# Two feed-forwards joined with the norms and the projection in front of them, in a four-block cross-attention network

## The reference

```python
def _L0_xattn_ref(...):
    ...                                   # x = x + causal self and context attention of _ln(x)
    hdn = _ln(_ln(x, g2, be2), gf, bf) @ w1 + b1          # w1: 256 x 1024
    hdn = jax.nn.gelu(hdn, approximate=False)
    x = x + (hdn @ w2 + b2)                               # w2: 1024 x 256
...
def _L3_xattn_ref(...):
    ...                                   # out = attention over ctx_1024
    attention = out @ w_out + b_out
    x = layernorm(attention + query, g1, beta1)
    ff = jax.nn.relu(x @ w_ff1 + b_ff1) @ w_ff2 + b_ff2
    return layernorm(ff + x, g2, beta2)
```

## Time and profile before

| what | value |
|---|---|
| median of 3 runs | 1797.35 us (1794.04 to 1807.53) |
| profiled execution | 1802.82 us, its span 1801.1 us |
| TensorE busy | 1422.7 us, 79% of the span |
| VectorE, ACT, GpSimd busy | 1046.8, 746.6, 514.5 us |
| mean granted TensorE clock | 0.873 of full speed |

### The profile page before, as it was taken

The page is one execution under the profiler, slowest core; times in us unless marked ns, Lnnn a source line. Parts: engine busy times, 40 slices in busy tenths (PEclk is TensorE's granted clock), DMA queues, the critical chain, the costliest instruction groups (busy, mean ns, idle before and its releaser), DMA issues. The chain is left out here.

```text
span 1801.1 us, 23058 instructions
## 1 busy us (share of the span) xinstructions
PE 1422.7 (79%) x7752; PEld 833.6 (46%) x7752; DVE 1046.8 (58%) x2359; ACT 746.6 (41%) x1044; POOL 514.5 (29%) x304
## 2 busy tenths in 40 slices
PE   5869998999369878769889668598895777587597
...
DMA packets 78127, 110.40 MB, mean 61 GB/s; under 512 B 16383, under 2 KB 55481, under 8 KB 76217
## 3 DMA queue, kind: packets, MB, share of 16 engines
...
...
## 5 line engine op out<-in xcount | busy, mean ns | idle before, releaser
L1036 PE MATMUL banks<-stacks 128*128 128x512 f32 (+4 forms) x640 | 252.9, 429 | 61.3 <-SPq L262 21.3
L1163 ACT ACTIVATE x_feat<-banks,key_bias 128x1024 f32<-128x1024 f32 x160 | 176.6, 1113 | 287.8 <-PE banks L1075 229.2
L1001 POOL TENSOR_TENSOR x_feat<-x_feat 128x1024 f32<-128x1024 f32 x112 | 265.6, 2372 | 87.5 <-ACT x_feat L1163 81.1
L1090 PE MATMUL banks<-x_feat,v_group 128*64 128x512 f32 (+4 forms) x1312 | 235.4, 574 | 10.1 <-ACT x_feat L1163 6.9
L1163 ACT ACTIVATE x_feat<-banks 128x1024 f32<-128x1024 f32 (+3 forms) x224 | 180.3, 839 | 142.8 <-PE banks L1069 93.5
L1206 DVE TENSOR_REDUCE max_parts<-banks 128x1 f32<-128x512 f32 (+3 forms) x384 | 192.9, 552 | 24.2 <-PE banks L1040 12.7
L1036 PEld LDWEIGHTS banks<-stacks 96*128 96x128 bf16 (+1 forms) x640 | 92.3, 148 | 239.9 <-DVE max_parts L1206 87.3
L1066 PE MATMUL banks<-stacks 99*128 99x512 bf16 (+3 forms) x512 | 141.1, 349 | 13.5 <-DMA stacks<-neg_max_parts 6.0
L1200 DVE CUSTOM_DVE_ANT_0 scratch<-banks,mask_rows 128x512 f32<-128x512 f32 x128 | 88.4, 691 | 67.4 <-PE banks L1036 67.2
L1074 PE MATMUL banks<-stacks 128*128 128x512 f32 x256 | 112.5, 440 | 7.1 <-DMA stacks<-neg_max_parts_r 7.1
L434 POOL TENSOR_TENSOR y_tok<-y_tok,rows_even 128x1024 f32<-128x1024 f32 x4 | 9.6, 2407 | 377.8 <-ACT y_tok L444 377.8
...
## 6 DMA issues: line engine op xcount, KB each, us to landing
...
```

What stands on the lines that cost most here:

```text
L1001: e.tensor_tensor(total, total, p, ALU.add)
L1036: m = e.matmul(PS[:, bank, at:at + wide], q[0:rows, h, qt * P:(qt + 1) * P], keys[0:rows, h, k0:k0 + wide], start=True, stop=not diag, ski ...
L1090: m = e.matmul(PS[w * h:w * (h + 1), bank, t.q0:CH], V[:, h, :], PB[:, t.index % 2, h // 2, h % 2, 0:CH - t.q0], start=t.first, stop=t.las ...
L1163: e.activation(dst, PS[:, 2 * (st % 2):2 * (st % 2) + 2, 0:CH - t.q0], ACT.Exp, scale=A.scale, bias=bias).then_inc(s.p_ready, 1)
```

## The change

Each of the two feed-forwards becomes one stage with what stands in front of it: three barriers fewer. Only chunk 0 goes through norms and transposes before the first hidden product (in the last block the projections of chunks 0 and 1, and the norm of chunk 0). What later chunks need is called by a function `between(c, m)` of each engine, after the step m of chunk c. Transposes and projections there use bank 3 alone, one at a time; the hidden products rotate over banks 0 to 2. The weight splits go in halves, and GpSimd's subtraction in pieces of 512 columns. The final norm's square root stands behind step 4 instead of 5, its normalisation behind 5 instead of 6. The context products' second pair moves to banks 4 and 5. The diff, cut to its core:

```diff
 
-    def split_weights_scalar(e, s, w):
-
-        for i in range(8):
+    def split_high(e, s, w, half):
+
+        for i in range(4 * half, 4 * half + 4):
             a = slice(CH * i, CH * (i + 1))
             h = e.activation(W_H[:, a], w[:, a], ACT.Copy)
         h.then_inc(s.w_high, 1)
 
-    def split_weights_gpsimd(e, s, w):
-        e.wait_ge(s.w_high, 1)
-        e.tensor_tensor(W_L, w, W_H.bitcast(F32), ALU.subtract)
-
-    def split_tokens_scalar(e, s, c):
+    def split_low(e, s, w, half):
+
+        e.wait_ge(s.w_high, half + 1)
+        for i in range(4 * half, 4 * half + 4):
+            a = slice(CH * i, CH * (i + 1))
+            h = e.tensor_tensor(W_L[:, a], w[:, a], W_H[:, a].bitcast(F32), ALU.subtract)
+        h.then_inc(s.w_low, 1)
+
+    def split_tokens_scalar(e, s, tn, c):
 
         if c < NC:
+            e.wait_ge(tn.taken, KT * (c + 1))
             need(e, s.hid_product, (c - 1) * MT_F)
             e.activation(XH[:, c % 2], XTF[:, :, c * CH:(c + 1) * CH], ACT.Copy).then_inc(s.x_high, 1)
 
@@ -1318,26 +1323,30 @@
             e.tensor_tensor(XL[:, c % 2], XTF[:, :, c * CH:(c + 1) * CH], XH[:, c % 2].bitcast(F32), ALU.subtract)\
                 .then_inc(s.x_split, 1)
 
-    def ffn_tensor(e, s):
+    def ffn_tensor(e, s, sp, between):
 
         w1h, w1l = (w[:, 0:2048].rearrange("p (k n) -> p k n", k=KT) for w in (W_H, W_L))
         w2h, w2l = (w[:, 2048:4096].rearrange("p (m n) -> p m n", m=MT_F) for w in (W_H, W_L))
 
         def hidden(i):
             c, m = divmod(i, MT_F)
-            need(e, s.hid_high, i - 3)
+            need(e, s.hid_high, i - 2)
+            if i == 0:
+                e.wait_ge(sp.w_low, 1)
             if m == 0:
                 e.wait_ge(s.x_split, c + 1)
             ms = slice(m * P, (m + 1) * P)
             for k in range(KT):
                 for w, x in ((w1h, XH), (w1h, XL), (w1l, XH)):
-                    mm = e.matmul(PS[:, i % 4, :], w[:, k, ms], x[:, c % 2, k, :],
+                    mm = e.matmul(PS[:, i % 3, :], w[:, k, ms], x[:, c % 2, k, :],
                                   start=k == 0 and w is w1h and x is XH, stop=k == KT - 1 and w is w1l)
             mm.then_inc(s.hid_product, 1)
 
         def second(i):
             c, m = divmod(i, MT_F)
             e.wait_ge(s.hid_split, i + 1)
+            if i == 0:
+                e.wait_ge(sp.w_low, 2)
             if m == 0:
                 need(e, s.added, 2 * (c - 1))
             for t in range(4):
@@ -1351,67 +1360,301 @@
         for i in range(n + 3):
             if i < n:
                 hidden(i)
+                between(*divmod(i, MT_F))
             if i >= 3:
...
+    def add_sums(e, s, c):
+        e.wait_ge(s.hid_used, (c + 1) * MT_F)
+        for k in range(2):
+            x = X[:, 4 * c + 2 * k:4 * c + 2 * k + 2, :]
+            e.tensor_tensor(x, x, PS[:, 4 + 2 * (c % 2) + k, :].rearrange("p (t d) -> p t d", t=2), ALU.add)\
+                .then_inc(s.added, 1)
+
+    def add_row_to(e, c, r):
+        e.tensor_tensor(four(X, c), four(X, c), wide(r), ALU.add)
+
+    def turn_alone(e, s, c, ks, src):
+
+        for k in ks:
+            need(e, s.taken, 2 * c + k)
+            for j in range(4):
+                t = e.transpose(PS[:, 3, j * P:(j + 1) * P], src[:, 4 * c + j, k * P:(k + 1) * P], ID[:, :])
+            t.then_inc(s.turned, 1)
+
+    BOTH = range(KT)
+
+    def take_alone(e, s, c, ks, cols):
+
+        for k in ks:
+            e.wait_ge(s.turned, 2 * c + k + 1)
+            scale, bias = cols or (None, None)
+            e.activation(XTF[:, k, c * CH:(c + 1) * CH], PS[:, 3, :], ACT.Identity,
+                         scale=1.0 if scale is None else COL[:, scale + k:scale + k + 1],
+                         bias=0.0 if bias is None else COL[:, bias + k:bias + k + 1]).then_inc(s.taken, 1)
+
+    def gain_gpsimd(e, s, c, g, dst):
+        e.wait_ge(s.normed, c + 1)
+        e.tensor_tensor(four(dst, c), four(Y3, c), wide(g), ALU.mult).then_inc(s.weighted, 1)
+
+
+    def first_ffn_tensor(e, s, sp, cs, nf, tn):
+
+        context_tensor(e, cs)
+        e.wait_ge(nf.normed, 1)
+        turn_alone(e, tn, 0, BOTH, Y3)
+        e.wait_ge(cs.keys_ready, 1)
+        e.wait_ge(cs.values_ready, B)
+        def between(c, m):
+            if m in (4, 5) and c + 1 < NC:
+                e.wait_ge(nf.normed, c + 2)
+                turn_alone(e, tn, c + 1, (m - 4,), Y3)
+        ffn_tensor(e, s, sp, between)
+
+    def first_ffn_scalar(e, s, sp, cs, n2, nf, tn):
+
+        cols = (COLS["gf"], COLS["bf"])
+        split_high(e, sp, W0_FF, 0)
+        square_root(e, n2, 0)
+        normalise(e, n2, 0, X, Y3, "layer")
+        split_high(e, sp, W0_FF, 1)
+        context_keys_scalar(e, cs)
+        square_root(e, n2, 1)
+        square_root(e, nf, 0)
+        normalise(e, nf, 0, Y3, Y3, "layer")
+        normalise(e, n2, 1, X, Y3, "layer")
+        context_values_scalar(e, cs)
+        take_alone(e, tn, 0, BOTH, cols)
+        split_tokens_scalar(e, s, tn, 0)
+        def between(c, m):
+            if m == 1 and c + 2 < NC:
+                square_root(e, n2, c + 2)
+            if m == 2 and c + 1 < NC:
+                square_root(e, nf, c + 1)
+            if m == 3 and c + 1 < NC:
+                normalise(e, nf, c + 1, Y3, Y3, "layer")
+            if m == 4 and c + 2 < NC:
+                normalise(e, n2, c + 2, X, Y3, "layer")
+            if m in (5, 6) and c + 1 < NC:
+                take_alone(e, tn, c + 1, (m - 5,), cols)
+            if m == 6 and c + 1 < NC:
+                split_tokens_scalar(e, s, tn, c + 1)
+        ffn_scalar(e, s, ACT.Gelu, COLS["L0f"], between)
+
+    def first_ffn_vector(e, s, zs, n2, nf):
+
+        statistics, scales, add_bias = ln_steps(e, n2, X, "layer", 1e-5, add=Y3, weighted=(Y3, row(RA, ROWS_L0, "be2")))
+        statistics_f, scales_f, _ = ln_steps(e, nf, Y3, "layer", 1e-5)
+        b2 = row(RA, ROWS_L0, "b2")
+        def second_norm(c):
+            add_bias(c)
+            e.drain()
+            statistics_f(c)
+        statistics(0)
+        scales(0)
+        statistics(1)
+        second_norm(0)
+        scales(1)
+        scales_f(0)
+        add_row_to(e, 0, b2)
+        split_tokens_vector(e, s, 0)
+        def between(c, m):
+            if m == 0 and c + 2 < NC:
+                statistics(c + 2)
+            if m == 1 and c + 1 < NC:
+                second_norm(c + 1)
+            if m == 2 and c + 1 < NC:
+                scales_f(c + 1)
+            if m == 3 and c + 2 < NC:
+                scales(c + 2)
+            if m == 4 and c > 0:
+                add_sums(e, s, c - 1)
+            if m == 5 and c + 1 < NC:
+                add_row_to(e, c + 1, b2)
+            if m == 6 and c + 1 < NC:
+                split_tokens_vector(e, s, c + 1)
+            if m == 7 and c == 0:
+                zeros_vector(e, zs)
+        ffn_vector(e, s, between)
+        add_sums(e, s, NC - 1)
+
+    def first_ffn_gpsimd(e, sp, cs, zs, n2):
+
+        g2 = row(RA, ROWS_L0, "g2")
+        split_low(e, sp, W0_FF, 0)
+        for c in range(NC):
+            gain_gpsimd(e, n2, c, g2, Y3)
+            if c == 0:
+                split_low(e, sp, W0_FF, 1)
+            if c == 1:
+                context_gpsimd(e, cs)
+        zeros_gpsimd(e, zs)
+
+
+    def last_ffn_tensor(e, s, sp, to, sq, nm, tz):
+
+        def free(turned_out, projected, turned_z):
+            need(e, to.taken, turned_out)
+            need(e, sq.taken2, projected)
+            need(e, tz.taken, turned_z)
+
+        def turn(ts, c, ks, counts):
+            for k in ks:
+                free(counts[0] + (k if ts is to else 0), counts[1], counts[2] + (k if ts is tz else 0))
+                for j in range(4):
+                    t = e.transpose(PS[:, 3, j * P:(j + 1) * P], Y3[:, 4 * c + j, k * P:(k + 1) * P], ID[:, :])
+                t.then_inc(ts.turned, 1)
+
+        def turn_out(c, ks, turned_z):
+            turn(to, c, ks, (2 * c, 2 * c, turned_z))
+
+        def turn_z(c, ks, turned_out):
+            e.wait_ge(nm.normed, c + 1)
+            turn(tz, c, ks, (turned_out, turned_out, 2 * c))
+
+        def project_out(c, p, turned_z):
+            free(2 * c + 2, 2 * c + p, turned_z)
+            for i in range(2):
+                t = 4 * c + 2 * p + i
+                for k in range(KT):
+                    m = e.matmul(PS[:, 3, i * D:(i + 1) * D], XTF[:, k, t * P:(t + 1) * P], W3.out[:, k, :],
+                                 start=k == 0, stop=k == KT - 1, skip_group_check=True)
+            m.then_inc(sq.product2, 1)
+
+        for c in range(2):
+            turn_out(c, BOTH, 0)
+            project_out(c, 0, 0)
+            project_out(c, 1, 0)
+        turn_z(0, BOTH, 4)
+        def between(c, m):
+            if m in (0, 1) and c + 2 < NC:
+                turn_out(c + 2, (m,), 2 * c + 2)
+            if m in (3, 4) and c + 2 < NC:
+                project_out(c + 2, m - 3, 2 * c + 2)
+            if m in (5, 6) and c + 1 < NC:
```

(113 more changed lines are left out.)

157 lines of the change are left out of this document (43 added, 114 removed).

## The result

The changed kernel took 1838.39 us (median of 4 runs, 1828.24 to 1839.72) beside 1797.55 us before: a ratio of 1.020, 95% interval 1.0166 to 1.0234. A second measurement of the same kernel on another chip gave 1826.78 us and 1.018 (1.0132 to 1.0229). Single executions of both measurements lie at 1826 to 1828 us or at 1838 to 1840: one of four at the lower place in the first, three of four in the second, with a mean granted clock of 0.875 to 0.881 there and 0.871 to 0.873 at the upper place. Forecast were 1820 us, 1790 to 1840. The profiled execution has a span of 1836.8 us, 35.7 more than the one of before.

A forecast was written before the change was run, and what follows sets the result against it. TensorE was taken to bound the feed-forwards, a chain over VectorE, ACT and GpSimd most of the fronts. First block -29 + 24 + 3 = -2, last -23 + 43.4 + 4 = +24: 1797.35 + 22.7 = 1820 us, range 1790 to 1840.

The forecast's parts named there:

- The fronts: Work ahead of each feed-forward's first hidden product: TensorE starts 29 us earlier in the first block, 23 in the last.
- (a): Second transpose of a pair waits in the single bank for ACT's take: 2.4 us, or 2.2 for attention's output.
- (b): Token split makes TensorE wait inside the feed-forwards: 3.4 us three times in the last block, 0.5 three times in the first.
- (c): Transposes and projections added to TensorE inside the feed-forwards: 3.1 us in the first block, 12.4 in the last.
- (d): First block, transpose in block 4 waits for ACT's late second norm: 6.5, 3.4 and 2.2 us in chunks 0 to 2.
- (e): Last block, the finished chunk's norm delays ACT's takes: waits become 5.2 us in chunk 1, 7.8 in chunk 2; surplus 8.2.
- A VectorE step waits for the GpSimd instruction that it meets: Fronts: a two-tensor VectorE step waits for the running GpSimd instruction, one 1.1 us piece; 2 us put for such waits.
- The clock: TensorE's clock falls in long pauses: 3 us lost in the first block, 4 in the last, between 0 and 12 together.
- the fourth: Rival: the low clock stays through whole chunks, +15 us, 1835 to 1850; chance 15%.
- my own forecast's 1810 to 1835: Third case, the prediction's own forecast of the kernel's time, 1810 to 1835 us; chance 50%.
- The second rival: ACT gets ahead between pauses, so (d), (e) and the clock are small: about 20 us less, 1800; chance 27%.
- The first, that handovers can be hidden: Rival: TensorE passes the waits of (a), (b), (d), (e) without loss, -36 us, 1761; chance 8%.

The follow-up runs named there:

- last_takes: Changed kernel, with ACT in the last block taking each transpose one step earlier: 1808.08 us, 1.004 of the kernel before.
- two_banks: Changed kernel, with hidden products over banks 0 and 1, transposes and projections over banks 2 and 3: 1795.32 us, 0.996 of the kernel before.
- last_all: Changed kernel; in the last block takes a step earlier, final norm a step later, token split behind step 6: 1796.30 us, 0.999 of the kernel before.
- first_relu: Changed kernel, with Relu in place of Gelu in the first feed-forward, so its ten table loads go: 1820.68 us, 1.011 of the kernel before.
- last_norm: Changed kernel, with the final norm's square root and normalisation again behind steps 5 and 6: 1819.07 us, 1.011 of the kernel before.
- one_piece: Changed kernel, with GpSimd's subtraction as one instruction a half instead of four pieces: 1833.83 us, 1.018 of the kernel before.
- both_mended: Changed kernel, with the last block's projection a stage of its own and both blocks' queues reordered: 1764.71 us, 0.979 of the kernel before.

## Why the prediction was right, and where it was short

Sign, place and mechanism were right; two sizes were off, in opposite directions, and that they partly cancelled is luck. Step by step, with what the profile after shows:

- The fronts. First block 27 us after the stage's start forecast, 26.9 measured. Last block 28 forecast, 31.7 measured: the projections and transposes there run at half clock for most of the time (three of four projections 3.75 to 3.78 us for 1.96), which I had put at 2 us.
- (a) 2.4 and 2.2 us a wait forecast; 2.12 and 1.84 measured. Shown to be the single bank and ACT's order by last_takes and two_banks, either of which removes it.
- (b) 3.4 us forecast in the last block, 3.04 measured; 0.5 forecast in the first block, 0.2 measured.
- (c) 3.1 and 12.4 us of added work forecast, too much: I had added durations of rows, and neighbouring rows overlap. The changed kernel's last feed-forward at full clock:

```profile
1730.22 1.55 PE L1341 MATMUL banks<-stacks 128*128 128x512 f32 x6
1731.61 1.89 PE L1540 MATMUL banks<-w_even,x_feat 128*128 128x256 f32 x8
...
1734.77 1.56 PE L1341 MATMUL banks<-stacks 128*128 128x512 f32 x6
1736.16 0.60 PE L1525 MATMUL banks<-ident,y_tok 128*128 128x128 f32 x4
...
1738.04 1.55 PE L1341 MATMUL banks<-stacks 128*128 128x512 f32 x6
```

  A step with a projection takes 4.55 us, one with a group of four transposes 3.27, one without 2.82: 1.73 and 0.45 us more. Six such groups in the first block are 2.7 us; ten groups and four projections in the last are 11.4. last_all leaves 12.7 over with one pause of 1.84 in it.
- (d) 6.5, 3.4, 2.2 forecast; 6.51, 3.06, 1.77 measured. The table loads' part is shown by first_relu.
- (e) 5.2 and 7.8 forecast; 4.71 and 7.30 measured; shown by last_norm. I had not carried it on into chunk 3, where the same late norm delays the last low parts, 1.76 us at the end.
- A VectorE step waits for the GpSimd instruction that it meets: shown by one_piece in the first block, and for a step with one tensor too.
- The clock is the term that was mis-sized. Forecast 3 and 4 us in the two feed-forwards. Measured: the first is 29.0 us longer, its pauses of over 0.2 us sum to 18.3 and its added work is 2.7, which leaves 8.0; the last is 54.6 longer, its pauses sum to 29.0 and its work is 11.4, which leaves 14.2. So 22 us of lower clock, not 7, and 3 more in the front; the changed kernel's second profile has 9.3 and 10.4, some 20. I had charged it to three pauses of 5 us and more; the rows show it also behind the pauses of 3 us in front of the last block's hidden products and behind two waits of 2.12 in the first block (2.91 and 2.86 us for 1.60), and so twice within a chunk: 2.81 and 1.97 us behind the pause of 4.71, then 1.77 and 2.76 behind the 3.04 that follows, for 1.60 and 1.55. What decides whether the clock falls behind a pause is not shown: behind 3.06 us in the first feed-forward it did not.

The sum: pauses and work were forecast at 67.3 us and came to 61.4; the clock inside the feed-forwards was forecast at 7 and came to 22; the fronts gave 4 us less than forecast. The two block sums were thus -2 and +24, and came to -0.2 and +35.4 (second profile +0.9 and +32.0). Of the rivals, the fourth had the amount of the first measurement and in part the reason (the granted clock was 0.85 to 0.92 over the last block's chunks, not half), while the second measurement lies in my own forecast's 1810 to 1835. The second rival (ACT catches up) is refuted by the pauses of (d) and (e), which came nearly as forecast. The first, that handovers can be hidden, is wrong for this kernel. both_mended saves 33 to 35 us where that rival had 36, but it is not the same kernel with other handovers: its projection stands apart again, and its queues are reordered.

The prediction's sentence on the Trainium skill, page "ScalarE: Activation LUTs", section "What ACT_TABLE_LOAD costs", gave 2.66 us for a table switch with its drain. Here the loads took 1.28 us and the next activation started at once; the first feed-forward grew by 29.0 us, where my terms had 27 and the page's drains, 10 x 1.38 us as an estimate, would have added up to 13.8 more. The measurement decides against the drain in this kernel.

What stays open: why the granted clock of the same stage differs from one execution to the next (0.79 and 0.88 in the rows of the window attention), which is most of the difference between the two profiles of the changed kernel; and which pauses the clock falls behind.
